# Layer 1's edge stage: a batch's four one-hots move to ScalarE, and TensorE loads its block numbers once per five batches

## The chip, the cores and the metric

The kernel runs on one core of one Trainium2 chip. The metric is the device time of one execution, in microseconds (us). The core has five engines that run their own instruction streams and meet at semaphores: TensorE (PE; its weight loads are listed apart as PEld), VectorE (DVE), ScalarE (ACT), GpSimd (POOL) and SyncE (SP, here a queue of DMA issues).
## The reference, cut to what matters

The program is a network of four layers on a graph of 3125 nodes with 256 features and 50000 edges. Layer 1's graph part is an attention over edges with four heads of 64 features:

```python
x_l = (x @ W_l + b_l).reshape(N, H, C)
x_r = (x @ W_r + b_r).reshape(N, H, C)
e = x_l[src] + x_r[dst] + (ea @ W_e).reshape(-1, H, C)
e = jnp.where(e > 0, e, NEG_SLOPE * e)
logits = jnp.einsum('ehc,hc->eh', e, att)
m = jax.ops.segment_max(logits, dst, num_segments=N)
a = jnp.exp(logits - m[dst])
denom = jax.ops.segment_sum(a, dst, num_segments=N)
out = jax.ops.segment_sum(x_l[src] * (a / denom[dst])[..., None], dst, num_segments=N)
```

The change touches only how the kernel finds, for each edge, the row of its destination node: as a one-hot row of 128 columns, one column for each node of a block of 128.

## The kernel before, in words

The edges are sorted by destination into 110 batches (NB) of four tiles (BATCH) of 128 edges. Two tiles make a pair, and the two pairs of a batch each belong to one block of 128 nodes. The number of that block is read at run time from a row in on-chip memory, `block_row`. Buffers for a batch stand in a ring of five (RING).

Each engine runs the same loop over batches, written with `skewed`: it takes pairs of a lag and a step. At iteration t an engine does each step for the batch t minus its lag, in the order written. The first five iterations and the last few are written out; the 105 between run as 21 trips of a loop over five iterations each, in which addresses and semaphore targets come from registers. The order inside an iteration is fixed by hand. In layer 1 (four heads, so `UNITS` is 2) it is:

- POOL (`L1Logits.gather`): `hot_tiles` of batch t (copy the source numbers to integers, L1027; one-hots of tiles 0 and 1, L1029), `gather_batch` of t (four indirect DMAs that fetch rows of the table, L995), `multiply` of t-2 (two products with the attention vector, L3355).
- DVE: `hot` of t-1 (`hot_half`: one-hots of tiles 2 and 3 in one instruction, L1037); `tops_of` for the first pair of t-4 (two reductions of 128x512, L3082); `raise_first` (L3090); `early` of t-3 (add the gathered rows, L3333); `tops_of` for the second pair; `raise_second` (L3097, L3099, L3102); `middle` of t-3 (L3333, then two L3338); `add(0)` of t-5 (four L3123); `fall` of t-4 (L3107, L3110); `add(1)` of t-5; `late` of t-3 (two reductions to logits, L3360).
- TensorE: `turn_logits(1)` of t-3; `add` of t-4 (L3179); `blocks` of t-1 (two `block_of`, each a register load from `block_row`, L1080, with its range check); `spread` of t-3 (L3185), which waits for `raise_second` on DVE and releases `fall`; `tensor` of t-1 (L3323, L3324), which takes the weights' block by the loaded number; `turn_logits(0)` of t-2 (L3165, L3168), which waits for DVE's first L3360 and releases the first `tops_of` reduction of DVE's next iteration; `turn` of t (L3150), the transpose of the one-hots.
- ACT: `shrinks` of t-3 (L3211); `weigh` of t-3 (one exponential of the powers, L3215, after `fall`; then 16 scaled copies L3224 and four L3226); `turn` of t (L3206, L3207); `flush` of t-4 (L3240, L3241 twice, each with its own register load at L1080).

SP loads the edge records of a batch as soon as the batch three behind has let go of its buffer.

## Time and profile before

| | |
|---|---|
| median of 3 runs | 6672.8 us (6668.49 to 6675.32) |
| the profiled execution | 6665.2 us, its span 6663.6 us |
| layer 1's edge stage in the span | 2439.8 to about 3530 us |
| busy in the span | PE 4995.6 us (75%), DVE 4271.6 (64%), ACT 2701.6 (41%), POOL 3055.4 (46%) |
| batches in the stretch from 2500 to 3496 us | 103 |

The page gives busy time by engine over the whole program, which is a mean over stages with different limits. For this change one stage counts, so the stretches, groups and order of time below are of that stage. "idle before" in a group is the time for which the engine stood still just before those instructions, and behind the arrow stands what ended most of it. An instruction can start a little before the one ahead of it on its engine has ended, so durations that are added up can exceed the elapsed time.

### The profile page before, as it was taken

To read this page: it belongs to the slowest core of one execution; us is meant where nothing else is said; L and a number is where in the kernel's file an instruction comes from. 1 tells how busy PE (TensorE), PEld (TensorE's weight loads), DVE (VectorE), ACT (ScalarE), POOL (GpSimd) and SP (SyncE) were. 2 spreads that over 40 slices of the span, in tenths; PEclk is the share of its full clock that TensorE was granted. 3 is DMA by queue.
4 is the path that set the end of the run, shared out by engine and by line. 5 is a ranking of instruction groups with operands and counts; after the bars stand their busy time and mean duration, and the time that the engine had idled before them with its cause. 6 is when DMAs were issued, how large, how long until landed. Compare 5 with 4: busy or idle time off the path is not lost. (4 is left out here: it accounts for less than half of the span.)

```text
span 6663.6 us, 121851 instructions
## 1 busy us (share of the span) xinstructions
PE 4995.6 (75%) x25924; PEld 3756.6 (56%) x25925; DVE 4271.6 (64%) x13455; ACT 2701.6 (41%) x7732; POOL 3055.4 (46%) x3657
## 2 busy tenths in 40 slices
PE   4740799995384378888883899949988997888594
PEld 3530567674252256666663666635655775666484
DVE  7772688884495579999996777743432114888603
ACT  0010677773013326666662111114523332888321
POOL 1777777776553028888880111033220000777212
PEclk8565999997595589999995899979988998999697
DMA  9221444454595212222231455534520001666453
GB/s 375 60 68 43 111 120 120 121 118 103 112 285 138 63 49 70 68 68 69 69 67 50 159 190 189 179 99 120 146 60 15 14 9 45 161 160 160 78 173 112
DMA packets 854768, 735.80 MB, mean 110 GB/s; under 512 B 405100, under 2 KB 756600, under 8 KB 854210
## 3 DMA queue, kind: packets, MB, share of 16 engines
q1 hardware_dynamic: 629890, 371.48, 20.2%
q0 software_dynamic: 118768, 280.68, 15.9%
q10 hardware_dynamic: 105936, 81.69, 3.7%
q8 instruction: 62, 1.02, 0.1%
q14 instruction: 112, 0.92, 0.0%
HBM read 520.38 MB, written 213.11 MB: 110 GB/s over the span
## 5 line engine op out<-in xcount | busy, mean ns | idle before, releaser
L995 POOL DMA_INDIRECT l3e_rows<-table,l3e_idx x440 | 433.0, 984 | 787.7 <-DVE l3e_idx L1017 659.3
L995 POOL DMA_INDIRECT l0e_rows<-table,l0e_idx x440 | 436.1, 991 | 120.8 <-issue 100.7
L995 POOL DMA_INDIRECT l1e_rows<-table,l1e_idx x440 | 430.5, 978 | 121.4 <-issue 121.4
L3224 ACT ACTIVATE l1e_weighted<-l1e_rows,l1e_power 128x64 f32<-128x64 f32 x1760 | 463.0, 334 | 14.7 <-ACT l1e_power L3215 7.3
L768 POOL DMA_INDIRECT records_by_src<-l0n_rec_src,l0n_pos_at_src x390 | 400.7, 1028 | 115.3 <-issue 109.0
L1266 PE MATMUL l0e_ps_w<-l0e_wf,l0e_hidT 128*128 128x256 f32 x1760 | 409.9, 386 | 0.3 <-PE l0e_ps_s L1277 0.3
L1266 PEld LDWEIGHTS l0e_ps_w<-l0e_wf,l0e_hidT 128*128 128x128 f32 x1760 | 325.8, 190 | 124.0 <-issue 84.1
L3165 PE MATMUL l1e_ps_row<-net_ident,l1e_logit 128*128 128x128 f32 x1760 | 277.8, 281 | 126.7 <-DVE l1e_logit L3360 125.7
L2069 DVE SCALAR_TENSOR_TENSOR net_x<-l2fe_ps_y,l2f_mix,net_x 128x256 f32 x200 | 96.8, 484 | 425.0 <-PE l2fe_ps_y L1996 364.4
L2032 ACT ACTIVATE l2fe_hT<-l2fe_ps_h,l2fe_own,l2fe_own 128x320 f32<-128x320 f32 x320 | 197.6, 618 | 314.0 <-PE l2fe_ps_h L1984 314.0
L2601 ACT ACTIVATE l1fg_hT<-l1fg_ps_h,l1fg_b_cols 128x256 f32<-128x256 f32 x256 | 107.5, 471 | 526.3 <-PE l1fg_ps_h L2546 526.2
L3179 PE MATMUL l3e_ps_s<-l3e_weighted,l3e_onehot 128*128 128x257 f32 x880 | 245.2, 422 | 93.7 <-ACT l3e_weighted L3226 93.7
L3355 POOL TENSOR_TENSOR l1e_e<-l1e_e,l1x_att 128x512 f32<-128x512 f32 x220 | 274.5, 1269 | 85.9 <-DVE l1e_e L3338 85.7
L3165 PEld LDWEIGHTS l1e_ps_row<-net_ident,l1e_logit 128*128 128x128 f32 x1760 | 193.1, 138 | 207.5 <-issue 154.2
L3725 PE MATMUL l2d_ps<-l2d_wide,net_work 128*128 128x512 f32 (+2 forms) x800 | 288.8, 516 | 7.9 <-DVE l2d_wide L3776 5.6
L3082 DVE TENSOR_REDUCE l1e_tile_top<-l1e_ps_row 128x2 f32<-128x512 f32 x440 | 287.3, 684 | 5.8 <-PE l1e_ps_row L3168 4.2
L2546 PE MATMUL l1fg_ps_h<-l1fg_xT,l1fg_w_in 128*128 128x256 f32 x1024 | 265.0, 381 | 1.7 <-DVE l1fg_xT L2638 0.8
L3323 PE MATMUL l1e_ps_x<-l1x_xr,l1e_nodehot 128*128 x880 | 257.7, 395 | 2.7 <-ACT l1e_nodehot L3207 2.7
L3179 PEld LDWEIGHTS l3e_ps_s<-l3e_weighted,l3e_onehot 128*128 128x128 f32 x880 | 158.8, 200 | 160.7 <-ACT l3e_weighted L3226 145.2
L2694 POOL COPY l1fg_now<-l1f_token_of 128x2 int32 (+1 forms) x32 | 5.9, 185 | 513.5 <-PE l1fg_ps_t L2535 484.6
L3643 POOL DMA_DIRECT2D l2d_counts<-counts x192 | 108.1, 564 | 277.5 <-ACT l2d_wide L3835 135.6
L2560 PE MATMUL l1fg_ps_y<-l1fg_w_out,l1fg_hT 128*128 128x256 f32 x1024 | 231.2, 379 | 0.0
(786 smaller groups left out, 14894.2 us busy)
## 6 DMA issues: line engine op xcount, KB each, us to landing
counts<-l1f_total ACTq DMA_DIRECT2D x272, 128.0 KB, 4.5
l1fg_w_in<-in_L_ffn_W SPq DMA_DIRECT2D x32, 1024.0 KB
l1fg_w_out<-in_L_ffn_W SPq DMA_DIRECT2D x32, 1024.0 KB
records_by_dst<-l0n_blank_dst SPq DMA_DIRECT2D x1, 32560.0 KB
l3e_rec<-records_by_dst SPq DMA_DIRECT2D x110, 296.0 KB
l2d_counts<-counts SPq DMA_DIRECT2D x208, 128.0 KB, 2.8
l2d_counts<-counts POOLq DMA_DIRECT2D x192, 128.0 KB, 2.7
l3fg_w_in<-in_L_ffn_w SPq DMA_DIRECT2D x16, 1024.0 KB, 5.3
```

Of the source, the lines that this page charges most:

```text
L768: pool.indirect_dma_start(self.to.records, bass.IndirectOffsetOnAxis(self.pos_at[b][:, j:j + 1], 0), at(self.rec[b], j, self.to.width), No ...
L995: pool.indirect_dma_start(at(self.rows[b], k, self.width), None, self.table, bass.IndirectOffsetOnAxis(self.idx[b][:, k:k + 1], 0)).then_i ...
L1266: ins = pe.matmul(ps_w[:, k, m * D:(m + 1) * D], hidT[b][:, c * WIDE + (2 * k + m) * P:c * WIDE + (2 * k + m + 1) * P], at(wf2, c, D), sta ...
L2546: ins = pe.matmul(ps_h[:, n % HALVES, (m % 2) * SLICE:(m % 2 + 1) * SLICE], w_in[b][:, c * F + m * P:c * F + (m + 1) * P], at(xT[b], c, SL ...
L2560: ins = pe.matmul(ps_y[:, t, 0:D], hT[b][:, c * SLICE + t * P:c * SLICE + (t + 1) * P], at(w_out[b], c, D), start=c == 0, stop=c == FC - 1)
L3082: dve.tensor_reduce(tile_top[:, c:c + w], tiled(ps_row[:, side, 0:w * PAIR], PAIR), AX.X, ALU.max)\
L3165: pe.matmul(ps_row[:, side, lo:lo + P], logit[b][:, c:c + 1].to_broadcast([P, P]), net.ident[:, :], is_transpose=True, start=h == h0 and m ...
L3179: ins = pe.matmul(ps_s[:, k, 0:W], at(g.onehot[b], m, P), at(weighted, m, W), start=m == 2 * k, stop=m > 2 * k)
L3224: act.activation(out[:, h, 0:each], g.rows[b][:, lo:lo + each], ACT.Copy, scale=power[b][:, m * heads + h:m * heads + h + 1])
L3323: pe.matmul(out, at(self.nodehot[b], 2 * k + m, P), at(self.xr, self.block[k], D), start=True, stop=False)
L3355: pool.tensor_tensor(e, e, self.att[:, :].unsqueeze(1).to_broadcast([P, 2, D]), ALU.mult).then_inc(self.times_att, 1)
L3725: ins = pe.matmul(ps[0:k_in, n % 2, 0:width(g)], lhsT, wide[k % WIDE][:, 0:width(g)], start=t == 0, stop=False)
```

## The change

POOL no longer makes one-hots: `hot_tiles` is replaced by `find_apart`, which keeps the copy of the source numbers. DVE no longer makes any: its `hot` step is gone in layer 1. ACT gets a new first step in its iteration, `mark` of batch t, which calls `hot_from_distance`: for each of the four tiles one ACTIVATE that writes |column number - node number| to a new buffer `away` (function Abs, the node number as a bias of one value per partition), then a wait for these four by ACT itself, and one ACTIVATE over all 512 columns that writes max(0, 1 - distance). TensorE waits for one semaphore instead of two before `turn`.

TensorE's `blocks` no longer loads two numbers in every iteration of the loop. In the first of the five iterations of a trip it loads ten at once with one call, and the other four take theirs from registers. In the written-out iterations it loads two as before. The range check of each number stays. Layer 3 uses the same edge function and gets nothing of this: `UNITS` is 1 there.

```diff
--- before.py
+++ after.py
@@ -966,7 +966,7 @@
         self.rec_loaded = [s.sem(f"rec_loaded{b}") for b in range(RING)]
         self.idx_ready = s.sem("idx_ready")
         self.hot_ready = s.sem("hot_ready")
-        self.half_ready = s.sem("half_ready")
+
         self.rows_loaded = [s.sem(f"rows_loaded{b}") for b in range(RING)]
         self.rec_free = s.sem("rec_free")
         self.rows_free = s.sem("rows_free")
@@ -1016,28 +1016,25 @@
         eng.wait_ge(self.rec_loaded[b], i * 16 + 16)
         eng.tensor_copy(self.idx[b][:, :], self.column(b, self.placed.far)).then_inc(self.idx_ready, 1)
 
+    def find_apart(self, eng, q, i, b, tick):
+
+        eng.wait_ge(self.rec_loaded[b], i * 16 + 16)
+        eng.sem_inc(tick, 1)
+        eng.tensor_copy(self.idx[b][:, :], self.column(b, self.placed.far)).then_inc(self.idx_ready, 1)
+
     def hot(self, eng, q, i, b):
         eng.wait_ge(self.hot_free, q + 1)
         mark_nodes(eng, self.net, self.onehot[b], self.column(b, self.placed.near)).then_inc(self.hot_ready, 1)
 
-    def hot_tiles(self, eng, q, i, b, tick):
-        eng.wait_ge(self.rec_loaded[b], i * 16 + 16)
-        eng.wait_ge(self.hot_free, q + 1)
-        eng.sem_inc(tick, 1)
-        eng.tensor_copy(self.idx[b][:, :], self.column(b, self.placed.far)).then_inc(self.idx_ready, 1)
-        for k in range(BATCH // 2):
-            ins = eng.tensor_scalar(at(self.onehot[b], k, P), self.net.columns[:, :], self.column(b, self.placed.near, k),
-                                    None, ALU.is_equal)
-        ins.then_inc(self.hot_ready, 1)
-
-    def hot_half(self, eng, q, i, b):
-        wide = [P, BATCH // 2, P]
-        eng.wait_ge(self.rec_loaded[b], i * 16 + 16)
-        eng.wait_ge(self.hot_free, q + 1)
-        eng.tensor_tensor(tiled(self.onehot[b][:, :], P)[:, BATCH // 2:BATCH, :],
-                          self.net.columns[:, :].unsqueeze(1).to_broadcast(wide),
-                          self.column(b, self.placed.near)[:, BATCH // 2:BATCH].unsqueeze(2).to_broadcast(wide), ALU.is_equal)\
-            .then_inc(self.half_ready, 1)
+    def hot_from_distance(self, act, q, i, b, away, away_ready):
+
+        act.wait_ge(self.rec_loaded[b], i * 16 + 16)
+        act.wait_ge(self.hot_free, q + 1)
+        for k in range(BATCH):
+            ins = act.activation(at(away, k, P), self.net.columns[:, :], ACT.Abs, bias=self.column(b, self.placed.near, k), scale=-1.0)
+        ins.then_inc(away_ready, 1)
+        act.wait_ge(away_ready, q + 1)
+        act.activation(self.onehot[b][:, :], away[:, :], ACT.Relu, bias=1.0, scale=-1.0).then_inc(self.hot_ready, 1)
 
     def wait_rows(self, eng, i, b):
         eng.wait_ge(self.rows_loaded[b], i * 16 * BATCH + 16 * BATCH)
@@ -1078,6 +1075,13 @@
 def block_of(eng, placed, pair):
 
     return eng.value_load(placed.block_row[0:1, bass.ds(pair, 1)], min_val=0, max_val=NT - 1)
+
+
+def blocks_of_round(net, engine, placed, first, n):
+
+    _, blocks = net.nc.values_load_multi_w_load_instructions(placed.block_row[0:1, bass.ds(first, n)], engines=[engine],
+                                                             min_val=0, max_val=NT - 1)
+    return blocks
 
 
 def open_sums(net, pe, ps, opens):
@@ -3130,7 +3134,7 @@
                                               zip((3, 3, 3, 0, 1), logits.vector_steps()))
             ends = (add(0), (4, fall), add(1), late) if UNITS > 1 else (late, hot, (4, fall), add(0), add(1))
             if UNITS > 1:
-                skewed(dve, hot, *units[:UNITS], (4, raise_first), early, *units[UNITS:], (4, raise_second), middle, *ends)
+                skewed(dve, *units[:UNITS], (4, raise_first), early, *units[UNITS:], (4, raise_second), middle, *ends)
             else:
                 skewed(dve, find, *units, (4, raise_first), early, (4, raise_second), middle, *ends)
 
@@ -3143,8 +3147,7 @@
 
             def turn(q, i, b):
                 pe.wait_ge(g.hot_ready, q + 1)
-                if UNITS > 1:
-                    pe.wait_ge(g.half_ready, q + 1)
+
                 pe.wait_ge(nodehot_ready, q + 1)
                 for k in range(BATCH):
                     ins = pe.transpose(at(ps_hot, k, P), at(g.onehot[b], k, P), net.ident[:, :])
@@ -3188,7 +3191,7 @@
                 ins.then_inc(spread_top, 1)
 
 
-            skewed(pe, *([(3, turn_logits(1))] if UNITS > 1 else []), (4, add), (1, lambda q, i, b: logits.blocks(pe, q)), (3, spread),
+            skewed(pe, *([(3, turn_logits(1))] if UNITS > 1 else []), (4, add), (1, lambda q, i, b: logits.blocks(pe, q, b)), (3, spread),
                    (1, lambda q, i, b: logits.tensor(pe, q, i, b)), (2, turn_logits(0)),
                    *([(2, turn_logits(1))] if UNITS == 1 else []), (0, turn))
 
@@ -3240,7 +3243,8 @@
                         act.activation(at(tops, blk, heads), top_at(b, k), ACT.Copy).then_inc(flushed, 1)
                     act.activation(at(net.work, blk, W), total[k][:, :], ACT.Copy).then_inc(flushed, 1)
 
-            skewed(act, (3, shrinks), (3, weigh), (0, turn), (4, flush))
+            mark = [(0, lambda q, i, b: logits.mark(act, q, i, b))] if UNITS > 1 else []
+            skewed(act, *mark, (3, shrinks), (3, weigh), (0, turn), (4, flush))
 
 
 class L1Logits:
@@ -3259,6 +3263,8 @@
         self.we_parts = s.sb("we_parts", [P, D], BF16)
         self.attrT = [s.sb(f"attrT{b}", [P, BATCH * P], BF16) for b in range(RING)]
         self.e = [s.sb(f"e{k}", [P, 2 * D]) for k in range(TWO)]
+        self.away = s.sb("away", [P, BATCH * P])
+        self.away_ready = s.sem("away_ready")
         self.loaded = s.sem("we_loaded")
         self.split_step = s.sem("split_step")
         self.parts_laid = s.sem("parts_laid")
@@ -3280,14 +3286,17 @@
         sp.dma_start(self.attrT[b][:, :], self.net.attr_parts[bass.ds(q * P, P), :]).then_inc(self.attr_loaded[b], 16)
 
     def gather(self, pool):
-        skewed(pool, (0, lambda q, i, b: self.g.hot_tiles(pool, q, i, b, self.pool_tick)), (0, lambda q, i, b: self.g.gather_batch(pool, q, b)),
+        skewed(pool, (0, lambda q, i, b: self.g.find_apart(pool, q, i, b, self.pool_tick)), (0, lambda q, i, b: self.g.gather_batch(pool, q, b)),
                (2, lambda q, i, b: self.multiply(pool, q)))
 
     def find(self, dve, q, i, b):
         pass
 
     def hot(self, dve, q, i, b):
-        self.g.hot_half(dve, q, i, b)
+        pass
+
+    def mark(self, act, q, i, b):
+        self.g.hot_from_distance(act, q, i, b, self.away, self.away_ready)
 
     def start_vector(self, dve):
         dve.sem_inc(self.x_read, TWO)
@@ -3307,8 +3316,14 @@
     def start_scalar(self, act):
         pass
 
-    def blocks(self, pe, q):
-        self.block = [block_of(pe, self.g.placed, q * TWO + k) for k in range(TWO)]
+    def blocks(self, pe, q, b):
+        if isinstance(q, int):
+            self.block = [block_of(pe, self.g.placed, q * TWO + k) for k in range(TWO)]
+            return
+        if b == RING - 1:
+            self.of_trip = blocks_of_round(self.net, mybir.EngineType.PE, self.g.placed, q * TWO, RING * TWO)
+        n = (b + 1) % RING
+        self.block = self.of_trip[n * TWO:(n + 1) * TWO]
 
     def tensor(self, pe, q, i, b):
 
@@ -3944,7 +3959,7 @@
     def start_scalar(self, act):
         pass
 
-    def blocks(self, pe, q):
+    def blocks(self, pe, q, b):
         pass
 
     def tensor(self, pe, q, i, b):
```

## Rows read from the trace of the kernel before

**Rows 1.** Stretch, us; busy PE, PEld, DVE, ACT, POOL; PE clock; DMA share; GB/s.

```profile
2500.00:3496.00 996.00, 864.03 (x5346) 669.76 (x5344) 933.45 (x2571) 687.60 (x2881) 815.34 (x926) 1.00 0.28 68
```

**Rows 2.** Groups of instructions from 2500 to 3496 us.

```profile
L3082 DVE TENSOR_REDUCE l1e_tile_top<-l1e_ps_row 128x2 f32<-128x512 f32 x412 | 268.7, 684 | 1.2
L3165 PE MATMUL l1e_ps_row<-net_ident,l1e_logit 128*128 128x128 f32 x1648 | 257.2, 279 | 110.7 <-DVE l1e_logit L3360 110.3
...
L1029 POOL TENSOR_SCALAR l1e_onehot<-net_columns,l1e_rec 128x128 f32<-128x128 f32 x206 | 145.2, 713 | 0.0
...
L3360 DVE TENSOR_REDUCE l1e_logit<-l1e_e 128x8 f32<-128x512 f32 x206 | 140.7, 683 | 26.0 <-POOL l1e_e L3355 24.0
...
L3206 ACT ACTIVATE l1e_outside<-l1e_ps_hot 128x512 bf16<-128x512 f32 x103 | 61.5, 597 | 19.0 <-ACT l1e_weighted L3226 19.0
...
L1037 DVE TENSOR_TENSOR l1e_onehot<-net_columns,l1e_rec 128x256 f32<-128x256 f32 x103 | 42.8, 416 | 0.0
...
L3215 ACT ACTIVATE l1e_power<-l1e_power 128x16 f32<-128x16 f32 x103 | 22.2, 216 | 221.8 <-DVE l1e_power L3110 221.8
```

**Rows 3.** Instructions in order of time, 3014.9 to 3017.7 us: start, duration.

```profile
3015.06 1.47 DVE L3360 TENSOR_REDUCE l1e_logit<-l1e_e 128x8 f32<-128x512 f32 x2
...
3015.88 0.65 PE L3165 MATMUL l1e_ps_row<-net_ident,l1e_logit 128*128 128x128 f32 x4 [1.17 <-DVE l1e_logit L3360]
...
3016.36 0.38 PE L3168 MATMUL l1e_ps_row<-l1e_outside,l1e_ident_bf 128*128 128x512 bf16 x1
...
3016.45 0.41 DVE L1037 TENSOR_TENSOR l1e_onehot<-net_columns,l1e_rec 128x256 f32<-128x256 f32 x1
...
3016.92 1.35 DVE L3082 TENSOR_REDUCE l1e_tile_top<-l1e_ps_row 128x2 f32<-128x512 f32 x2
```

**Rows 4.** Order of time where batches end and no one-hots are left, 3499.1 to 3501.9 us.

```profile
3499.24 0.68 DVE L3360 TENSOR_REDUCE l1e_logit<-l1e_e 128x8 f32<-128x512 f32 x1
...
3500.24 0.69 DVE L3360 TENSOR_REDUCE l1e_logit<-l1e_e 128x8 f32<-128x512 f32 x1 [0.32 <-POOL l1e_e L3355]
...
3501.11 0.69 DVE L3082 TENSOR_REDUCE l1e_tile_top<-l1e_ps_row 128x2 f32<-128x512 f32 x1 [0.18 <-PE l1e_ps_row L3168]
```

**Rows 5.** TensorE sequencer's L1080 from 3018.9 to 3020.6 us: ns min/median/max, first and last start.

```profile
L1080 PEldq FUSED_REGOPS  x4: 46/106/151, 3019.0 to 3020.2; - x4
...
L1080 PEldq TENSOR_LOAD <-net_block_row_dst x2: 299/299/299, 3019.1 to 3019.8; - x2
...
L1080 PEldq SEQ_ASSERT  x2: 18/18/18, 3019.7 to 3020.4; - x2
```

**Rows 6.** Register loads of SyncE's sequencer at L3635, in layer 2.

```profile
L3635 SPq TENSOR_LOAD <-net_cell_row x247: 262/270/293, 4471.2 to 4909.5; - x124
```

**Rows 7.** TensorE in order of time, 3018.8 to 3026.3 us.

```profile
3021.13 1.05 PE L3185 MATMUL l1e_ps_top<-l1e_top,l1e_nodehot 128*128 128x4 f32 x8 [0.18 <-DVE l1e_shrink L3102]
```

**Rows 8.** VectorE in order of time, 3015.0 to 3025.6 us.

```profile
3023.56 0.17 DVE L3107 TENSOR_TENSOR l1e_ps_top<-l1e_logit,l1e_ps_top 128x16 f32<-128x16 f32 x1
```

**Rows 9.** Groups of ScalarE in layer 0's edges, 560 to 1530 us.

```profile
L1308 ACT ACTIVATE l0e_raised<-l0e_raised,l0e_half 128x512 f32<-128x512 f32 x220 | 145.8, 715 | 0.0
...
L1305 ACT ACTIVATE l0e_raised<-l0e_raised 128x512 f32<-128x512 f32 x220 | 126.1, 628 | 0.0
...
L1290 ACT ACT_TABLE_LOAD x1 | 1.3, 1283 | 230.8 <-DVE l0e_bf L1191 230.8
```

**Rows 10.** Groups of ScalarE by shape over the span: Abs with a bias per partition.

```profile
L1451 ACT ACTIVATE l0u_raised<-l0u_ps_h,l0u_bo 128x128 f32<-128x128 f32 x50 | 15.5, 366 | 0.5 <-PE l0u_ps_h L1428 0.5
```

**Rows 11.** GpSimd in order of time where the stage starts, 2439 to 2462 us.

```profile
2440.00 1.37 POOL L1029 TENSOR_SCALAR l1e_onehot<-net_columns,l1e_rec 128x128 f32<-128x128 f32 x2
...
2446.56 1.20 POOL L1029 TENSOR_SCALAR l1e_onehot<-net_columns,l1e_rec 128x128 f32<-128x128 f32 x2
...
2452.88 1.20 POOL L1029 TENSOR_SCALAR l1e_onehot<-net_columns,l1e_rec 128x128 f32<-128x128 f32 x2
...
2459.08 2.49 POOL L3355 TENSOR_TENSOR l1e_e<-l1e_e,l1x_att 128x512 f32<-128x512 f32 x2
```

## Prediction before the run

> **What bounds the kernel now.** I read first the page, to see how much of the program layer 1's edge stage is: about 1090 of 6663.6 us. Then the busy time of the stretch in which it runs evenly. The 103 batches there take 996 us, 9.67 us each. VectorE is busy for 933 us of it (94%), TensorE for 864 us, at its full clock (granted 1.00, the 2.4 GHz level), GpSimd for 815 us and ScalarE for 688 us [rows 1]. By that table VectorE sets the time, and taking work from it should pay. But VectorE still stands idle for 6%, and busy time doesn't tell whether an instruction could have been left out without anything moving. So the groups come next, with their waits. In each batch TensorE waits 1.07 us (110.7 / 103) for the first logit reduction, and VectorE 0.25 us (26.0 / 103) for GpSimd's product before the second. The one-hots of VectorE take 0.416 us a batch, those of GpSimd two times 0.71 us. ScalarE waits 2.15 us (221.8 / 103) for the powers [rows 2].
>
> What decides is the order of time around the one-hots. The first logit reduction ends at 3015.06 + 0.68 = 3015.74 (the pair takes 1.47). TensorE turns these logits from 3015.88, its L3168 ends at 3016.36 + 0.38 = 3016.74, and VectorE's next reduction, which reads that result, starts 0.18 us later, at 3016.92 [rows 3]. So from the end of the first logit reduction to the first top reduction there are 1.18 us that belong to TensorE and to two hand-overs, whatever VectorE does meanwhile. What it does meanwhile is the second logit reduction and the one-hots, which end at 3016.45 + 0.41 = 3016.86 [rows 3]. They fill a hole. The group of the top reductions shows 1.2 us of idle time before 412 of them [rows 2]: hole and filling are equally long, to a few hundredths. The loop that sets the batch is therefore VectorE's own chain from the first top reduction to the first logit reduction, 8.5 us, and these 1.18 us of TensorE.
>
> The trace holds the case without the one-hots, too. Near the stage's end VectorE's `hot` has run out of batches. There the first logit reduction ends at 3499.92, the second at 3500.93, and the top reduction starts only at 3501.11, after a recorded wait of 0.18 us for TensorE: again 1.19 us after the first [rows 4].
>
> **VectorE loses its one-hots** (105 looped batches of 0.416 us). It starts the top reduction when TensorE is done, so it gains only what the one-hots were longer than the hole, a few hundredths at most: I take 0.01 us a batch, -1 us in all. Without TensorE's cover it would be 0.416 less the overlap of neighbours (L1037 starts 0.08 before L3360 ends), so 0.33 us a batch or 35 us. That is the other bound, nothing is the first; rows 4 choose between them.
>
> **GpSimd loses its one-hots** (1.42 us a batch). Its gathers start earlier, and its product then waits longer for the bends of VectorE, which it waits for already; the second logit reduction still waits for the product, inside the 1.18 us. Nothing in the steady part. At the start it is different: the first product stands behind three batches of copies, one-hots and gathers, and its start at 2459.08 is what VectorE's first logits wait for. Three pairs go from ahead of it, 1.37 + 1.20 + 1.20 = 3.8 us [rows 11]. -3.8 us, once.
>
> **ScalarE gets five instructions.** Abs over 128x128 with a bias per partition: 50 of them, two and two, take 15.5 us, which is 0.62 for two, one lasting 0.366 [rows 10]; four make 4 x 0.366 - 3 x 0.11 = 1.13, and 1.2 with some for the source in on-chip memory. Its wait for its own result: 0.18 (19.0 / 103) [rows 2]. The function over 128x512: 0.63 without a pointer operand, 0.715 with one [rows 9]. Together 2.0 us at most, with neighbours' overlap of 0.1 taken off. They stand ahead of `shrinks` and L3215, just where ScalarE now waits 2.15 us. Behind them in the queue are the exponential of the shrinks, which VectorE needs only in its next iteration, and that of the powers, which still comes in time by 0.15 us or more. If nothing overlaps, the five take 4 x 0.366 + 0.18 + 0.715 + 0.18 = 2.54 us, 0.3 more than the 2.25 there are (the wait and an overlap of 0.1): up to 31 us over 105 batches. I take nothing, as neighbours on ScalarE do overlap in rows 10. No table load comes in: in layer 0's edges Abs (L1302), an exponential (L1305) and a logarithm (L1308) take turns 220 times, with one load of 1.283 us for all [rows 9]. TensorE turns the one-hots after `turn_logits(0)`, and by then they are made: ScalarE makes them ahead of L3215, which runs before the logits of that iteration exist.
>
> **TensorE's block numbers.** This is the part that can cost. The sequencer is through its instructions well ahead of the array: it starts on L1080 at 3019.0, while `add` still runs. One number takes a register operation for the address (0.06), the load (0.30), the range check (0.151 + 0.018) and some 0.055 between each, 0.75 us; the last check starts at 3020.4 [rows 5]. `spread` begins at 3021.13, as soon as VectorE releases it [rows 7]. So the loads are hidden now in every batch: to remove them from four batches in five gains nothing. In the fifth, ten numbers are read and checked in one go ahead of `spread`. Address and load once are 0.47, ten checks 10 x 0.28 = 2.8: 3.3 us if the load costs no more for ten than for one. It ends at 3022.3, `spread` starts near 3022.4, 1.27 us late. VectorE's `fall` stands at 3023.56 [rows 8] and needs the end of `spread`, 3021.13 + 1.05 = 3022.18 [rows 7], plus a hand-over of 0.18: slack 1.20. So late by 0.07 us a trip; 21 trips, 1.5 us. `tensor`, behind `spread`, has the 1.07 us and a little more before `turn_logits(0)`, and comes out even.
>
> What a load of ten registers takes, no row shows. Below stands no more than one, 0.30 us for all. Above stands ten times one, 3.0 us. The nearest row is that of a single load: on SyncE's sequencer it is 0.270 [rows 6], and a register operation that reads no memory 0.046 [rows 5], so the read itself is some 0.22 us. Nothing in the trace shows two reads of one sequencer overlapping. I take 0.22 for each of the nine more: 2.0 us. Then `spread` is 3.25 us late, `fall` 3.25 - 1.20 = 2.05, and since VectorE's chain is the loop that sets the time, no later batch gives it back: 21 x 2.05 = +43 us. By the upper bound it is 21 x 2.77 = 58.
>
> The Trainium skill (Runtime: NRT & Kernel Launch, section on instruction fetch mechanics) says that a sequencer's register load costs about 200 ns per register even in bulk; it speaks of loads from HBM, and no row here shows a load of several registers. By that, as an estimate, the nine cost 1.8 us and the 21 trips 39 us instead of 43.
>
> **Sum**: -1 - 3.8 + 43 = +38 us. Against the profiled execution that is 6665.2 to 6703. The median of the runs is 7.6 us above the profiled one, and I add the difference to it: 6711 us.
>
> **The rivals.**
> - *The ten reads cost little more than one*: +1.5 - 4.8 = -3 us, 6669. For it: a row of 40 adjacent bytes could be read at once. Against it: the read is most of the single load's time. The two part at 0.09 us a register: there `fall` is 0.86 us late, which makes +18 - 5 = +13 us.
> - *VectorE's one-hots do set the time*, and the reads cost little: 105 x 0.33 = -35, with the start -39, 6635 us. It needs TensorE's answer to come earlier than 1.18 us once nothing is between. For it: VectorE is 94% busy. Against it: rows 4, which show the wait in its place.
> - *ScalarE becomes the bound*: five instructions above 2.25 us, up to +31 us on the case above, 6700 us with cheap reads. For it: the margin is 0.15 to 0.35 us of a batch, and at each trip's end ScalarE's branch comes on top. Against it: each term is a row.
> - The Trainium skill (ScalarE: Activation LUTs, rules for kernel authors) advises VectorE rather than ScalarE for a maximum and the like. That rival is its place here: 2.0 us of ScalarE stand for 0.416 + 1.42 us of the other two.
>
> **How the numbers follow.** Differences under 0.2% (13 us) can't be told from none here. Slow reads: 0.47. Cheap reads and all else hidden: 0.34. ScalarE as the bound: 0.08. VectorE's one-hots worth their time: 0.11. The forecast is the first, 6711 us; its own range goes from its threshold, 6686, to the upper bound's 6726. Since cases of both signs have weight, the range over them reaches from the cheap reads' 6669 less a few us to just above the upper bound: 6662 to 6728; the one-hots' gain and a slow ScalarE on top of slow reads are left out. Faster 0.11, the same 0.34, slower 0.55.
>
> **What would show it.** In the profile after: L3360 and L3082 with a wait for TensorE of about 0.3 us a batch where L1037 was; the end of the first logit reduction to the first top reduction at 1.18 still; L3215's wait down from 2.15 to some 0.2 us; a single register load of TensorE's sequencer each 48 us, of near 2.3 us, followed by ten checks of 0.28, `spread` late by 3 us in that batch and `fall` waiting for it for 2 us. A load of 0.3 to 0.5 us, or a first top reduction sooner than 1.1 us after the logits, would prove the forecast wrong.

## The result and the profile after

The kernel after takes 6744.94 us (median of 4 runs, 6742.89 to 6747.52), the one before 6670.65 beside it (4 runs, 6667.37 to 6675.32): a ratio of 1.0111 [1.0095, 1.0127], 74 us more. Forecast were 38 more, with 6728 as the upper end. The sign was right, the size was half of it. The profiled execution took 6744.27 us, its span is 6742.6. From the first number copied by GpSimd to the last sum, the stage lasted 1095.4 us before and 1166.1 after, so 70.7 of the 74 us between the medians (79 between the two profiled executions) arise in it. The rest of the program took 5568 us before and 5576 after, and 5575 to 5580 in the four profiles taken later on a chip like this one, with four different kernels.

A batch's period is the time from one batch's first top reduction (L3086 of the kernel after) to the next one's. Over the same 100 batches its mean went from 9.69 to 10.38 us, but not evenly. In a trip of five, four batches take 9.59, 9.86, 9.59 and 9.79 us (medians), and before they took 9.57, 9.84, 9.59 and 9.65. The fifth is the one in which TensorE loads ten numbers: its median is 12.7 us and its mean 13.0, where it took 9.69, and it varies from 10.3 to 15.0. Nearly the whole loss lies there: the 21 batches with a load are together 69.7 us longer than the same batches before, all the others together 2.7.

First the stretch and the groups that answer to [rows 1] and [rows 2], from the kernel after. Only 96 batches fit into these 996 us, where 103 did.

```profile
2500.00:3496.00 996.00, 839.38 (x4990) 651.08 (x4989) 848.84 (x2301) 813.51 (x3167) 621.95 (x672) 0.96 0.25 64
```

```profile
L3086 DVE TENSOR_REDUCE l1e_tile_top<-l1e_ps_row 128x2 f32<-128x512 f32 x384 | 251.4, 686 | 63.9 <-PE l1e_ps_row L3171 63.4
...
L3375 DVE TENSOR_REDUCE l1e_logit<-l1e_e 128x8 f32<-128x512 f32 x192 | 129.3, 682 | 20.4 <-POOL l1e_e L3370 18.5
...
L1034 ACT ACTIVATE l1e_away<-net_columns,l1e_rec 128x128 f32<-128x128 f32 x384 | 121.5, 387 | 1.8
...
L1037 ACT ACTIVATE l1e_onehot<-l1e_away 128x512 f32<-128x512 f32 x96 | 60.6, 632 | 3.0
...
L3218 ACT ACTIVATE l1e_power<-l1e_power 128x16 f32<-128x16 f32 x96 | 20.8, 216 | 91.9 <-DVE l1e_power L3114 91.9
...
L3111 DVE TENSOR_TENSOR l1e_ps_top<-l1e_logit,l1e_ps_top 128x16 f32<-128x16 f32 x96 | 16.5, 172 | 28.5 <-PE l1e_ps_top L3188 28.5
```

VectorE waits for TensorE at two places. Before the first operation of `fall` (L3111) it waits 28.5 us, where the wait was 0.0: the forecast named this one. Before the top reductions (L3086) it waits 63.9 us, where it was 1.2; the forecast expected 0.3 us a batch there, about 29. The rest is the part that it lacked, but for some 0.2 us in each batch with a load: there the product is ready early, and the 0.25 us that VectorE otherwise waits before its second logit reduction turn up at L3086 instead. TensorE's granted clock is 0.96 in the mean, where it was 1.00.

Now TensorE's sequencer in one trip, from 2742 to 2749 us of the kernel after (ns min/median/max, first and last start), and then the loads of all 19 trips in the stretch.

```profile
L1082 PEldq FUSED_REGOPS  x11: 60/146/151, 2742.5 to 2747.7; - x11
L1082 PEldq SEQ_ASSERT  x10: 18/18/18, 2745.4 to 2747.9; - x10
L1082 PEldq TENSOR_LOAD <-net_block_row_dst x1: 2411/2411/2411, 2742.7 to 2742.7; - x1
...
L1082 PEldq TENSOR_LOAD <-net_block_row_dst x19: 1083/2401/2418, 2534.6 to 3467.6; - x19
```

The load takes 2.41 us, the ten range checks run from 2745.1 to 2747.95, 0.28 us each, and only then comes `spread`. In the next trip the same load takes 1.09 us, and so they alternate: 11 trips with 1.09, 10 with 2.41. What TensorE and its clock do meanwhile, windows of 2 us and the order of time show (columns of the windows as in [rows 1]).

```profile
2744.00:2746.00 2.00, 0.49 (x3) 0.08 (x1) 1.87 (x6) 1.39 (x6) 0.95 (x1) 1.00 0.35 88
2746.00:2748.00 2.00, 0.00 (x0) 0.00 (x1) 1.19 (x5) 1.23 (x4) 1.39 (x2) 1.00 0.45 113
2748.00:2750.00 2.00, 2.00 (x11) 1.63 (x12) 0.83 (x5) 0.35 (x2) 1.23 (x2) 0.72 0.00 0
2750.00:2752.00 2.00, 2.00 (x7) 1.33 (x6) 1.57 (x4) 2.00 (x11) 1.65 (x2) 0.50 0.13 27
2752.00:2754.00 2.00, 2.00 (x15) 1.69 (x14) 0.16 (x1) 2.00 (x11) 1.39 (x3) 0.92 0.34 105
2754.00:2756.00 2.00, 2.00 (x17) 1.65 (x16) 1.86 (x4) 1.39 (x6) 0.80 (x1) 1.00 0.42 125
```

```profile
2744.41 0.22 DVE L3106 SCALAR_TENSOR_TENSOR l1e_shrink<-l1e_top,l1e_fresh 128x4 f32<-128x4 f32 x1
...
2745.22 1.28 ACT L1034 ACTIVATE l1e_away<-net_columns,l1e_rec 128x128 f32<-128x128 f32 x4
...
2748.00 1.07 PE L3188 MATMUL l1e_ps_top<-l1e_top,l1e_nodehot 128*128 128x4 f32 x8 [3.51 <-issue]
...
2749.11 0.18 DVE L3111 TENSOR_TENSOR l1e_ps_top<-l1e_logit,l1e_ps_top 128x16 f32<-128x16 f32 x1 [1.92 <-PE l1e_ps_top L3188]
...
2750.14 1.06 PE L3338 MATMUL l1e_ps_x<-l1x_xr,l1e_nodehot 128*128 x2
2750.30 1.27 DVE L3375 TENSOR_REDUCE l1e_logit<-l1e_e 128x8 f32<-128x512 f32 x2
...
2751.21 1.06 PE L3338 MATMUL l1e_ps_x<-l1x_xr,l1e_nodehot 128*128 x2
...
2752.84 0.60 PE L3168 MATMUL l1e_ps_row<-net_ident,l1e_logit 128*128 128x128 f32 x4
...
2753.84 1.33 DVE L3086 TENSOR_REDUCE l1e_tile_top<-l1e_ps_row 128x2 f32<-128x512 f32 x2 [2.27 <-PE l1e_ps_row L3171]
```

L3106, the last thing that `spread` waits for, ended at 2744.63. TensorE starts `spread` at 2748.00, 3.37 us after it where 0.06 is usual, and has stood still for 3.51 us with nothing awaited ("issue"). These 3.3 us of delay are the forecast's 3.25. Then the clock goes to 0.50. `tensor` (L3338) needs 1.07 us from one pair of matmuls to the next, and lasts from 2748.94 to 2752.84, 3.9 us. In the batch before that of 2798 it takes 2.25, with 0.55 from pair to pair. So `turn_logits(0)`, behind it, starts 1.9 us after the logits that it turns (the first L3375 ends at 2750.98), and VectorE stands for 2.27 us a second time. With the cheap load it is mostly the same: in the trip at 2795 TensorE pauses for 2.15 us only, VectorE's `fall` waits 0.54, but the clock is 0.52 and 0.62 in the windows from 2800 to 2804, `tensor` takes 3.93 us, and the top reduction waits 2.29.

Two of the 21 trips, at 2897 and 3416 us, show the delay without the clock. The first of them, around its `spread`:

```profile
2904.00:2906.00 2.00, 2.00 (x13) 1.58 (x14) 1.42 (x8) 1.02 (x6) 2.00 (x3) 1.00 0.23 55
2906.00:2908.00 2.00, 2.00 (x16) 1.64 (x15) 1.38 (x3) 2.00 (x11) 1.10 (x2) 1.00 0.00 0
```

```profile
2903.50 1.05 PE L3188 MATMUL l1e_ps_top<-l1e_top,l1e_nodehot 128*128 128x4 f32 x8 [2.14 <-issue]
...
2907.66 1.34 DVE L3086 TENSOR_REDUCE l1e_tile_top<-l1e_ps_row 128x2 f32<-128x512 f32 x2 [0.62 <-PE l1e_ps_row L3171]
```

The load (1.09 us), the pause (2.14) and the wait of `fall` (0.53) are those of the trip at 2795, but the clock stays at 1.00, `tensor` takes 2.25 us, and the top reduction starts 1.21 us after the first logit reduction has ended, nearly the usual 1.18. This batch takes 10.33 us (the other 10.37), the one at 2795 takes 12.01. So with the cheap load the delay costs 0.65 us of a trip, and the fallen clock 1.65 on top. Of the other nine trips with the cheap load eight take 11.9 to 12.1 us, and the first of all 13.7. In the ten trips with the dear load the clock always fell. Four of these batches take 13.3 to 13.4 us, and `fall` waits 1.9 to 2.1 in them. Six take 14.8 to 15.0: there most of `spread` itself ran at half clock (1.6 to 1.9 us instead of 1.05), and `fall` waits 2.5 to 2.7.

In a batch without loads, VectorE in order of time, to be held against [rows 3]:

```profile
2790.78 1.46 DVE L3375 TENSOR_REDUCE l1e_logit<-l1e_e 128x8 f32<-128x512 f32 x2
2792.64 1.34 DVE L3086 TENSOR_REDUCE l1e_tile_top<-l1e_ps_row 128x2 f32<-128x512 f32 x2 [0.40 <-PE l1e_ps_row L3171]
```

The first logit reduction ends at 2790.78 + 0.68 = 2791.46, the top reduction starts 1.18 us later. L1037 of VectorE is gone from between them, and the hole is as long as it was.

The start of the stage, GpSimd in order of time, against [rows 11]:

```profile
2437.05 0.19 POOL L1023 CAST l1e_idx<-l1e_rec 128x4 int32<-128x4 f32 x1 [338.62 <-DMA l1e_rec<-records_by_dst]
2438.07 0.97 POOL L995 DMA_INDIRECT l1e_rows<-table,l1e_idx  x1 [0.83 <-POOL l1e_idx L1023]
...
2454.39 2.48 POOL L3370 TENSOR_TENSOR l1e_e<-l1e_e,l1x_att 128x512 f32<-128x512 f32 x2
```

From the first copy to the first product it is 17.34 us, and was 19.26 (the first copy before stood at 2439.82). The gain is 1.9 us, not 3.8: the gathers now wait 0.81 us for the copy's result, which the one-hots had covered but for 0.16.

### The profile page after: what moved, and what is told of

Its sections match the earlier page's. It is cut to its first block and busy times, and to the rows that moved or that the text cites. A ratio compares the mean times of both kernels' runs of the same rounds, so it can differ in the third digit from the quotient of the medians.

```text
span 6742.6 us, 121629 instructions
## 1 busy us (share of the span) xinstructions
PE 5029.3 (75%) x25860; PEld 3791.6 (56%) x25925; DVE 4247.5 (63%) x13345; ACT 2898.4 (43%) x8282; POOL 2891.1 (43%) x3437
## 3 DMA queue, kind: packets, MB, share of 16 engines
q0 software_dynamic: 118768, 280.68, 15.6%
## 5 line engine op out<-in xcount | busy, mean ns | idle before, releaser
L3086 DVE TENSOR_REDUCE l1e_tile_top<-l1e_ps_row 128x2 f32<-128x512 f32 x440 | 288.4, 686 | 76.1 <-PE l1e_ps_row L3171 75.4
L3338 PE MATMUL l1e_ps_x<-l1x_xr,l1e_nodehot 128*128 x880 | 289.0, 431 | 2.7 <-ACT l1e_nodehot L3210 1.4
```

The lines of the kernel that those rows point to most:

```text
L3086: dve.tensor_reduce(tile_top[:, c:c + w], tiled(ps_row[:, side, 0:w * PAIR], PAIR), AX.X, ALU.max)\
L3338: pe.matmul(out, at(self.nodehot[b], 2 * k + m, P), at(self.xr, self.block[k], D), start=True, stop=False)
```

## The experiments

They ran in three groups, each beside the kernel before on the same chip. That kernel took 7552 us on the chip of the first group, 7492 on that of the second and 6669 on that of the third, which is like the chip of the result. Three explanations were open: that the loads and checks of ten numbers cost all of it by making TensorE late, that ScalarE's five instructions cost too, and that the part beyond the lateness is TensorE's clock.

**The two parts apart.** `act_only` is the change with `blocks` as before (two numbers in each batch); `blocks_only` is the kernel before with the load of ten.

```diff
     def blocks(self, pe, q, b):
-        ...
-        if b == RING - 1:
-            self.of_trip = blocks_of_round(self.net, mybir.EngineType.PE, self.g.placed, q * TWO, RING * TWO)
-        ...
+        self.block = [block_of(pe, self.g.placed, q * TWO + k) for k in range(TWO)]
```

> The change's one-hots on ScalarE, with TensorE's block numbers loaded two at a time in every iteration, as before. Theory A (the whole loss comes from TensorE's ten loads in one piece): within 0.2% of before, my sum without that part being -5 us; the first top reduction still starts 1.18 us after the first logit reduction ends, though VectorE has no one-hots. Theory B (ScalarE's five instructions cost time too): slower by 10 to 30 us. Theory C (VectorE's one-hots were worth their time, and the ten loads hid it): faster by 30 us or more.

> The kernel before with TensorE's ten loads at once alone; the one-hots stay on GpSimd and VectorE. Theory A: +70 to +80 us, as much as the whole change (+74), 3.5 us a trip. Theory B: +45 to +65 us, the rest being ScalarE's.

Against 7551.95 us, `act_only` took 7601.95 (1.0077 [1.0053, 1.0102]) and `blocks_only` 7630.63 (1.0100 [1.0064, 1.0135]). The load of ten costs without any change to the one-hots: mean period 10.56 us (9.75 for the kernel before there), and 13.2 in the batch with the load. But ScalarE's part cost 50 us as well, where the forecast has nothing, or 31 at the most. So it had to be repeated on a chip like the one of the result.

**The change without its checks** (`no_checks`): the ten range checks of each load are left out, the loads stay.

```diff
-    ..., engines=[engine], min_val=0, max_val=NT - 1)
+    ..., engines=[engine], min_val=0, max_val=NT - 1, skip_runtime_bounds_check_because="...")
```

> The change with the range checks of the ten numbers left out (the numbers are in range, so nothing computed changes). Ten checks took 0.28 us each on TensorE's sequencer. Theory A: what is left is a load of 2.4 or 1.1 us; it ends less than 0.6 us after VectorE's release of `spread`, inside the slack of 1.2 us, and TensorE stands idle too briefly for its clock to fall: equal to the run with two numbers at a time, within 0.2% of before. If it is the loads as such and not the length of the pause, 30 us or more are lost.

7592.66 us, 1.0057 [1.003, 1.0085]. Its stage lasted 1142.3 us, that of `act_only` 1142.8, and VectorE's wait at L3112 (`fall`) was 0.0 again: without the checks no load makes `fall` late. The loads are still not free. In six of the ten trips with the load of 2.41 us TensorE stood still for 1.45 us before `spread`, its clock fell (0.50 from 3308 to 3310 us), and the batch took 11.2 to 11.5 us; in the other four the clock stayed at 1.00 after a pause as long, and the batch took 9.7 to 10.4. The ten together are 11 us longer than at 9.7 each. Eight of the eleven trips with the load of 1.09 us take 9.7. On this chip, whose other pauses come below, the whole times can't tell 11 us from nothing. The checks are the larger half of the pause, and leaving them out took away most of what it costs.

**Loads of many sizes** (`load_sizes`): twenty loads of TensorE's sequencer ahead of the stage, without checks, in the kernel before.

> The kernel before, with twenty register loads of TensorE's sequencer put once ahead of the stage: 1, 2, 3, 4, 6, 8, 10 and 12 numbers from place 0 of the row, then 2 from places 1 and 2, 4 from 2 and 1, 8 from 2, 10 from 1, 2, 3, 4 and 8, then 10 from 2 and 0 again. In the change's profile loads of ten took 1.09 and 2.41 us in turn. Theory: the place decides. A load that starts at a multiple of four numbers (16 bytes) costs 1.09 for ten, one that starts two numbers off 2.41. Rival: it is the state of the machine at the moment (what else runs), and here all loads of ten cost about the same.

Nobody used the numbers and nothing checked them, and the loads were not in the program that ran. The run told nothing of loads. Its trace is that of the kernel before on the first group's chip (7547.23 us), and there it served below.

**The clock by itself.** `five_calls` loads the ten numbers in the same place by five calls of two. `five_calls_fed` puts three 128x128 matmuls of zeros into a spare part of PSUM between the calls, so that TensorE has work during the pause.

```diff
             self.of_trip = ()
             for k in range(RING):
+                if k:
+                    for _ in range(3):
+                        pe.matmul(self.spare, self.net.zeros[:, 0:P], self.net.zeros[:, 0:P], start=True, stop=True)
                 self.of_trip += tuple(blocks_of_round(self.net, mybir.EngineType.PE, self.g.placed, (q + k) * TWO, TWO))
```

> The change, with the ten numbers of a trip loaded in the same place by five calls of two instead of one call of ten. If a load of two costs about what one costs (0.3 us), the burst on TensorE's sequencer is about 5.2 us, as long as the change's slower one. Theory A (a pause of TensorE costs twice: `spread` comes late, and the clock falls to half for the matmuls behind it): `fall` late by about 2 us and 2 to 2.7 us more by the clock, in each of 21 trips: +85 to +100 us. Theory B (lateness alone): +45 us.

> The run with five calls, with three matmuls of zeros between each two calls, into columns of a PSUM bank that nobody reads. They add work and a little issue time (I expect about 1 us to the burst) and keep the array from pausing for over about 1 us. Theory A: the granted clock stays at 1.00 behind the burst and the first top reduction comes 1.18 us after the logits again; the trip loses 3 us instead of 4.3, +60 to +70 us, less than the run with five calls though it does more. Theory B: with more work it is slower than that run by about 20 us.

Against 7491.57 us: `five_calls` 7605.73 (1.0174 [1.0136, 1.0212]), `five_calls_fed` 7574.95 (1.0118 [1.0081, 1.0156]). A load of two takes 0.54 us, five of them 2.7, so five calls are no cure. What tells clock and lateness apart is the second. First windows around one trip and groups from 3100 to 4200 us of `five_calls`:

```profile
3306.00:3308.00 2.00, 0.00 (x0) 0.00 (x0) 2.00 (x6) 0.68 (x3) 0.47 (x1) 1.00 0.58 135
...
3312.00:3314.00 2.00, 2.00 (x7) 1.47 (x7) 1.62 (x7) 1.15 (x5) 1.39 (x2) 0.50 0.24 66
```

```profile
L3086 DVE TENSOR_REDUCE l1e_tile_top<-l1e_ps_row 128x2 f32<-128x512 f32 x402 | 263.5, 686 | 77.5 <-PE l1e_ps_row L3171 75.7 <-DMA l0ff_rec_dst<-in_edge_attr 1.4
...
L3111 DVE TENSOR_TENSOR l1e_ps_top<-l1e_logit,l1e_ps_top 128x16 f32<-128x16 f32 x101 | 17.6, 174 | 72.8 <-PE l1e_ps_top L3188 72.8
```

And the same of `five_calls_fed`:

```profile
3306.00:3308.00 2.00, 1.25 (x9) 1.07 (x9) 1.10 (x5) 1.62 (x5) 1.49 (x2) 1.00 0.43 105
...
3312.00:3314.00 2.00, 2.00 (x17) 1.67 (x16) 1.22 (x2) 2.00 (x11) 1.39 (x3) 1.00 0.28 94
```

```profile
L3087 DVE TENSOR_REDUCE l1e_tile_top<-l1e_ps_row 128x2 f32<-128x512 f32 x416 | 273.5, 686 | 56.7 <-PE l1e_ps_row L3172 50.3 <-issue 6.0
...
L3112 DVE TENSOR_TENSOR l1e_ps_top<-l1e_logit,l1e_ps_top 128x16 f32<-128x16 f32 x105 | 18.3, 174 | 62.8 <-PE l1e_ps_top L3189 62.8
```

More work for TensorE made the stage 37 us shorter (1221.4 to 1184.2). `spread` is as late as before (it starts 4.46 us after what it waits for, and 4.38 without the matmuls), but the clock stays at 1.00 where it was 0.50; from 3100 to 4200 us its mean rises from 0.94 to 0.99, and the median of the batch with the loads falls from 15.7 to 12.8 us. The matmuls hold the clock in 15 of the 21 trips only. In the other six it falls behind `spread`, and the batch takes 14.4 to 15.0 us: the same run again shows the price, about 1.65 us. So the delay and the clock are two causes. They do not part neatly by the two waits: 0.75 us of the wait before `fall` (3.72 and 2.97 us a trip) was the clock's too, as `spread` ran at half speed. And the gain is not all kept, since the batch behind the one with the loads takes 0.64 us more in the mean (10.23, and 9.59 without the matmuls); which of the added work does that was not looked into.

**The other way to gain**, found while the waits were read: the second logit reduction waits for GpSimd's product and stands in front of nothing urgent. `early_pairs` is the kernel before with `add(1)` between the two logit reductions, and a product that starts when its own pair is bent; `early_pairs_act` adds ScalarE's part of the change.

```diff
-            ends = (add(0), (4, fall), add(1), late) if UNITS > 1 else (late, hot, (4, fall), add(0), add(1))
+            late_of = [(3, lambda q, i, b, k=k: logits.vector_late(dve, q, i, b, (k,))) for k in range(TWO)]
+            ends = (add(0), (4, fall), late_of[0], add(1), late_of[1]) if UNITS > 1 else (late, hot, (4, fall), add(0), add(1))
...
-        pool.wait_ge(self.bent, q * TWO + TWO)
         pool.sem_inc(self.pool_tick, 1)
         for k in range(TWO):
+            pool.wait_ge(self.bent, q * TWO + k + 1)
```

> The kernel before, one-hots and loads as they were, with two orders changed: VectorE adds the second pair's sums between the two logit reductions instead of ahead of them, and GpSimd multiplies the first pair as soon as that pair is bent. If the hole between the first logit reduction and the first top reduction is what bounds a batch, the first reduction comes 0.95 us sooner, TensorE's 1.18 us lie under the sums, the second reduction and the one-hots, and VectorE becomes gapless: 9.67 to about 9.2 us a batch, -45 to -50 us. If VectorE's busy time were the bound as it stood, this would gain nothing, since nothing is taken from it.

> The same two orders on top of the change's one-hots on ScalarE (loads of TensorE two at a time). Here VectorE's missing one-hots should be worth their 0.33 us, because the hole is gone. But ScalarE had only about 0.45 us a batch left in the change's profile, and on the chip of the last runs it already stood in the way. Expected: no better than the run with GpSimd's and VectorE's one-hots, -30 to -50 us, with ScalarE busy for over 95% of the stage.

`early_pairs` took 7460.78 us (0.9967 [0.9946, 0.9988]), 31 us less than the kernel before where 45 to 50 were expected; mean period 9.46 us. `early_pairs_act` took 7479.49 (0.9991 [0.9971, 1.0012]), 9.67 us: not to be told from the kernel before, where 30 to 50 us less were expected, and slower by 0.2 us a batch than without ScalarE's part. ScalarE was busy for 87% of the time from 3200 to 4100 us, not for over 95%.

**On a chip like the first**: the whole change (`change_again`), ScalarE's part alone (`act_again`, the kernel of `act_only`), the twenty loads with their range checks (`load_places`), and a mixture (`early_pairs_half`): the two orders above, GpSimd keeps its two one-hots, and ScalarE makes only VectorE's two, with two Abs and one max(0, 1 - distance) over 256 columns.

```diff
+    def half_from_distance(self, act, q, i, b, away, away_ready):
+        ...
+        for k in range(BATCH // 2, BATCH):
+            ins = act.activation(at(away, k, P), self.net.columns[:, :], ACT.Abs, bias=self.column(b, self.placed.near, k), scale=-1.0)
+        ...
+        half = slice(BATCH // 2 * P, BATCH * P)
+        act.activation(self.onehot[b][:, half], away[:, half], ACT.Relu, bias=1.0, scale=-1.0).then_inc(self.half_ready, 1)
```

> The whole change once more, beside its ScalarE part alone on the same chip, since that part cost 0.8% where the sum had it at nothing. Theory A (two causes add: ten loads 60 to 75 us, ScalarE's part 0 to 60 us by the chip's instruction supply): the whole is slower than the part by 35 to 75 us. Theory B (the ten loads alone): the part is within 0.2% of before where ScalarE's sequencer shows no register operation of 0.7 us, as in the first profile of the change.

> The one-hots on ScalarE with TensorE's numbers loaded two at a time, a second time. Last time +0.77% on a chip where ScalarE's sequencer had register operations of 0.7 us (instead of 0.04), 11 batches over 10.5 us and TensorE's clock at 0.98 in the stage. If those pauses of the sequencer are the cause, a profile without them shows no batch over 10.5 us and a time within 0.2% of before; with them it repeats +0.5 to +0.8%.

> The kernel before, with twenty register loads of TensorE's sequencer, range checks and all, put once ahead of the stage: 1, 2, 3, 4, 6, 8, 10 and 12 numbers from place 0 of the row, then 2 from places 1 and 2, 4 from 2 and 1, 8 from 2, 10 from 1, 2, 3, 4 and 8, then 10 from 2 and 0 again. (Without the checks they had been dropped from the program as unused.) Theory: the place decides: ten from a multiple of four numbers (16 bytes) 1.09 us, ten from two numbers off 2.41. Rival: the moment decides, and all loads of ten are about alike.

> The two orders that gained 0.3% (sums between the logit reductions, product per pair), with GpSimd keeping its two one-hots and ScalarE making only VectorE's two. ScalarE gets 1.1 us a batch instead of 1.7, and VectorE loses 0.416. With the hole gone VectorE's 0.33 us should now be worth their time: 9.41 to about 9.1 us a batch, 30 to 40 us faster than that run, 60 to 80 us faster than before. If ScalarE's pauses bind again, it is no faster than that run.

Against 6668.83 us (15 runs, 6661.4 to 6676.02): `change_again` took 6741.06, 1.0108 [1.0092, 1.0123]; `act_again` 6674.16, 1.0007 [0.9997, 1.0016]. So on this chip ScalarE's part costs 5 us, no more than can be told from none, and the loads cost 67. The stretch and the groups of `act_again`, from 2500 to 3496 us:

```profile
2500.00:3496.00 996.00, 860.99 (x5334) 668.19 (x5333) 907.38 (x2459) 869.05 (x3381) 665.89 (x718) 1.00 0.27 68
```

```profile
L3086 DVE TENSOR_REDUCE l1e_tile_top<-l1e_ps_row 128x2 f32<-128x512 f32 x412 | 269.6, 686 | 26.7 <-PE l1e_ps_row L3171 25.7
...
L3218 ACT ACTIVATE l1e_power<-l1e_power 128x16 f32<-128x16 f32 x102 | 22.0, 216 | 43.0 <-DVE l1e_power L3114 43.0
...
L3111 DVE TENSOR_TENSOR l1e_ps_top<-l1e_logit,l1e_ps_top 128x16 f32<-128x16 f32 x102 | 17.2, 169 | 0.0
```

The clock is 1.00, `fall` waits for nothing, the top reductions wait 26.7 / 103 = 0.26 us a batch (forecast 0.3), and ScalarE is left with 43.0 / 102 = 0.42 us of its wait (forecast 0.2 or more).

Why did ScalarE's part cost on the other chips? Operations of ScalarE's sequencer take about 0.7 us there now and then, in the stage of every profile of the first and of the second group, and in none of the six profiles of the third group and of the result. The same 18 ns operation, in the stage, from `act_only` and then from `act_again`:

```profile
L1077 ACTq SEQ_ASSERT  x156: 17/18/728, 3169.2 to 3947.1; - x156
```

```profile
L1077 ACTq SEQ_ASSERT  x216: 18/18/18, 2482.7 to 3522.5; - x108
```

The trace of `load_sizes`, the kernel before on that chip, has them too (a register operation at L3241: 16/51/738 ns), so the change doesn't bring them. In `act_only` the loss sits in 17 batches of over 10.5 us, and in 12 of these TensorE's clock fell as well (mean under 0.75 in the 5 us from the start of `spread`); the kernel before has one batch of over 10.5 us there. The likely account is that 2.15 us of slack swallowed the pauses, that 0.42 us do not, and that TensorE's clock adds its price. It is not shown: no run here changed the pauses, and what they are stays open.

The loads of `load_places`, each a query of its own (ns, start). In order, (first number, how many): (0,1), (0,4), (0,8), (0,12), (2,4), (4,10), (2,10).

```profile
L3310 PEldq TENSOR_LOAD <-net_block_row_dst x1: 317/317/317, 2430.2 to 2430.2; - x1
...
L3310 PEldq TENSOR_LOAD <-net_block_row_dst x1: 365/365/365, 2433.8 to 2433.8; - x1
...
L3310 PEldq TENSOR_LOAD <-net_block_row_dst x1: 602/602/602, 2438.1 to 2438.1; - x1
...
L3310 PEldq TENSOR_LOAD <-net_block_row_dst x1: 869/869/869, 2445.1 to 2445.1; - x1
...
L3310 PEldq TENSOR_LOAD <-net_block_row_dst x1: 1000/1000/1000, 2451.8 to 2451.8; - x1
...
L3310 PEldq TENSOR_LOAD <-net_block_row_dst x1: 1091/1091/1091, 2476.4 to 2476.4; - x1
...
L3310 PEldq TENSOR_LOAD <-net_block_row_dst x1: 2412/2412/2412, 2484.4 to 2484.4; - x1
```

Where the first number's place is a multiple of four, four numbers cost little more than one (0.37 and 0.32 us) and each further four 0.24 to 0.27; numbers beyond the last full four cost 0.23 to 0.25 each (ten from 0, 4 or 8: 1.08 to 1.10 us). From the places 1, 2 and 3 each number costs about 0.24: two take 0.54, four from 1 or 2 take 1.00, ten take 2.40 to 2.41. The change's first number moves on by ten each trip, so every second trip has the cheap place. That is the alternation of 2.41 and 1.09.

`early_pairs_half` took 6610.23 us, 0.9914 [0.99, 0.9927]: 59 us less than the kernel before and 131 less than the change. VectorE in order of time:

```profile
3015.47 0.69 DVE L3368 TENSOR_REDUCE l1e_logit<-l1e_e 128x8 f32<-128x512 f32 x1
3016.07 0.85 DVE L3124 SCALAR_TENSOR_TENSOR l1e_total<-l1e_total,l1e_shrink,l1e_ps_s 128x65 f32<-128x65 f32 x4
3016.84 0.68 DVE L3368 TENSOR_REDUCE l1e_logit<-l1e_e 128x8 f32<-128x512 f32 x1
3017.44 1.28 DVE L3083 TENSOR_REDUCE l1e_tile_top<-l1e_ps_row 128x2 f32<-128x512 f32 x2
```

The hole after the first logit reduction is now 3017.44 - 3016.16 = 1.28 us, and it is full: four sums and the second reduction lie in it, with no wait. Mean period 9.12 us. That fits the view that VectorE's one-hots are worth nothing while they only fill a hole, and are worth their time once other work fills it: the two orders alone had 9.46 us in the second group, 0.34 more, and the one-hots take 0.33 once the overlap with their neighbour is taken off. But these are two chips. How much is each order's and how much ScalarE's was not run on one.

## Why the prediction was wrong in size

- **Reading of the bound**: right. The 1.18 us between the first logit reduction and the first top reduction are TensorE's; they stayed with the one-hots gone, and `act_again` shows a wait of 0.26 us a batch in their place.
- **VectorE's one-hots, -1 us**: right within what can be told; the mean period with ScalarE's part alone is 9.72 us, and was 9.69, since one batch of five takes 9.79 instead of 9.65.
- **Start of the stage, -3.8 us**: measured -1.9. The time of the removed instructions was counted, but not what they had covered, the gathers' wait for the copy.
- **ScalarE, 0 with up to +31 as a rival**: 0 on this chip. Four Abs take 1.28 us, the other 0.63 with a gap of 0.03 ahead of it, 1.9 in all. The wait of 0.18 us for its own result does not show in that gap. The Trainium skill (ScalarE: Activation LUTs, rules for kernel authors) advises against such work on ScalarE; on this chip the slack hid it. On the first group's chip it cost 50 us, and on the second's 19 on top of `early_pairs`: there ScalarE did cost time, but probably by its sequencer's pauses, and not by the sum of five instructions that the rival was built on.
- **The load of ten, 2.3 us**: 2.41 in every second trip, 1.09 in the others. The Trainium skill (Runtime: NRT & Kernel Launch, section on instruction fetch mechanics) has 200 ns a register even in bulk, for loads from HBM. Here, from on-chip memory, it is about 0.24 at three places in four, and 0.24 to 0.27 for four further registers at once at the fourth. The rival of cheap reads was half true, every second trip.
- **The lateness, 2.05 us x 21 = 43**: its working held for the trips with the dear load (`spread` 3.3 us late; `fall` waits 1.92 us where `spread` still ran at full clock). With the cheap load the whole delay costs 0.65 us, as the two trips at full clock show. For the dear load no trip kept its clock; the wait of 1.92 and the 0.10 us that a trip with the cheap load loses beyond its wait make 2.02, an estimate. 11 x 0.65 + 10 x 2.02 = 27.4 us.
- **The step that failed** is the sentence on what comes after `spread`: "`tensor`, behind `spread`, has the 1.07 us and a little more before `turn_logits(0)`, and comes out even". It took `tensor` at the length that it has at full clock. At full clock it holds even for the late `spread`: in the two trips without a fallen clock the top reduction comes 0.03 us later than usual. But TensorE had stood still for 2 to 3.5 us, in 19 of 21 trips the granted clock fell to 0.50 or near it, and `tensor` took 3.1 us or more, 3.9 in the trip shown, instead of 2.25; in seven trips most of `spread` was slow as well. What the 21 batches lost beyond the delay is 69.7 - 27.4 = 42 us, and the forecast had nothing for it. That it is the clock and not the delay is what the two trips show for the cheap load, and `five_calls_fed` for a longer pause.

The sum by measured terms: 27.4 (delay) + 42 (clock) - 1.9 (start) + 2.7 (the other batches) = 70 us, beside the 70.7 by which the stage grew, 74 between the medians and 72 in the third group. Without the clock's 42 it would be 28 and not the forecast's 38: the delay was taken 15.6 us too high, because every second load is cheap, against which 2 us of the start and 4 of the other batches were missing. So the forecast would have been too high by 10 us without the clock; as it was, the clock left it 36 us short of the 74.

The Trainium skill (TensorE: Matmul & The Clock Gate, section on HAM oscillation) describes the pattern: a kernel whose array waits in every round loses its clock in every round, and pays for it each time anew. This case's windows agree for 19 of 21 trips, 1.00 to 0.50 and back within 8 us in the one shown. It was not weighed in the forecast.

## What to carry to other kernels

Instructions of a sequencer that are spread out can be free, and the same ones in a row a pause of the engine: gathering them saved nothing in 84 batches and cost 3.3 us in each of 21. Ask of every pause of TensorE what its next matmuls cost at half clock, and who waits for them; here that was 42 us, and the delay itself 27. And where an engine's instructions fill a hole that another engine sets, removing them yielded nothing here; the fastest kernel of this case is one that first ordered other work into the hole.

## What the runs showed of the hardware

- A load of TensorE's sequencer into several registers from on-chip memory: four at once in 0.37 us from a place that is a multiple of four, 1.00 us from the place after it; ten in 1.09 or 2.41 us.
- A range check costs 0.28 us for each number loaded, so ten of them (2.85 us) cost more than their dear load.
- TensorE's granted clock fell from 1.00 to 0.50 after a pause of 2.15 us, as after one of 3.51, but not each time: in two trips of 21 it stayed at 1.00 after 2.14 and 2.18 us. Small matmuls on zeros in a longer pause kept it at 1.00 in 15 of 21 trips.
- Two chips took 12 to 13% more time for the kernel before. In every profile from these two chips single operations of ScalarE's sequencer lasted about 0.7 us now and then (up to 0.73 in `act_only`, one of 1.4 in `five_calls_fed`); in the six from chips like the first none did.
